# A scratch buffer of the memory stage laid out with the key innermost

## The reference

```
q = (xn @ w_q.T).reshape(b, n, 2, h, kd).transpose(2, 0, 1, 3, 4)
sim = jnp.einsum('pbnhd,hkpd->pbnhk', q, keys)      # 2 sides x 8 heads x 32 keys
s, i = jax.lax.top_k(sim, k)                        # 8 best of each side
all_scores = (sx[..., :, None] + sy[..., None, :]).reshape(b, n, h, k * k)
scores, pk = jax.lax.top_k(all_scores, k)           # 8 best pairs of each head
w_down = key_in[idx];  w_up = key_out[idx]
o = jnp.einsum('bnd,bnhkd->bnhk', inputs, w_down)
o = jax.nn.gelu(o, approximate=False) * jax.nn.softmax(scores, axis=-1)
return jnp.einsum('bnhk,bnhkd->bnd', o, w_up)
```

## Time and profile before

| what | value |
|---|---|
| median of 3 runs | 2622.75 us (2621.32 to 2628.96) |
| the profiled execution, its time | 2621.93 us |
| its span in the profile | 2620.1 us |
| granted TensorE clock over the span | 0.951 of full |
| busy over the span | PE 89%, DVE 79%, ACT 72%, PEld 71%, POOL 32% |

### The profile page before, as it was taken

One profiled execution on the slowest core, in us unless ns is written; L12 is line 12 of the kernel. 1 busy time (PEld: TensorE's weight loads), 2 busy tenths in 40 slices (PEclk: granted clock), 3 DMA queues, 4 the chain that ended last, 5 costly groups with the idle time before them and its releaser, 6 DMA issues.

```text
span 2620.1 us, 95472 instructions
## 1 busy us (share of the span) xinstructions
PE 2343.8 (89%) x34892; PEld 1855.1 (71%) x34892; DVE 2078.6 (79%) x5455; ACT 1887.8 (72%) x3592; POOL 836.3 (32%) x1203
## 2 busy tenths in 40 slices
PE   2999943966999999999889999899899999999999
PEld 1676632645888888888857667566688788888887
DVE  6788889668899999999667777688766777777776
ACT  1888852777688888878467777788567777777776
POOL 1455510336566666666333333233100000000000
PEclk9999975987899999999899999899799999999999
DMA  5000000000000000000020000111011111111111
GB/s 183 1 0 0 0 17 1 1 0 3 2 0 0 0 0 0 0 0 0 3 66 0 0 0 0 36 43 44 30 43 46 49 56 52 57 51 54 52 57 45
DMA packets 56808, 64.82 MB, mean 25 GB/s; under 512 B 7696, under 2 KB 35088, under 8 KB 56592
## 3 DMA queue, kind: packets, MB, share of 16 engines
q1 hardware_dynamic: 56720, 63.65, 7.9%
HBM read 59.17 MB, written 4.46 MB: 24 GB/s over the span
## 4 chain that ended last, share of the span: by engine, by line
PE 68%; DVE 17%; issue 9%; ACT 2%; SPq 1%; DVEq 1%; POOL 1%; ACTq 0%; POOLq 0%; DMA 0%
PE ps L1075 5%; PE ps L1118 5%; PE ps L1103 5%; PE ps L1348 4%; PE ps L1370 4%; PE ps L1372 4%; PE ps L1371 4%; PE ps L1350 4%; PE ps L1349 4%; PE ps L1131 3%; PE ps L1090 3%; DVE work L1829 2%; PE ps L1248 2%; DVE work L1830 2%; DVE work L1836 2%
## 5 line engine op out<-in xcount | busy, mean ns | idle before, releaser
L559 POOL TENSOR_TENSOR work<-work,consts_sb 128x1024 f32<-128x1024 f32 x128 | 245.9, 1921 | 387.8 <-ACT work L727 346.9
L1260 PE MATMUL ps<-work 32*32 32x32 f32 x16384 | 249.5, 224 | 45.7 <-DVE work L1779 31.6
L1260 PEld LDWEIGHTS ps<-work 32*32 32x32 f32 x16384 | 242.2, 145 | 60.3 <-issue 60.3
L1988 DVE TENSOR_TENSOR h_low<-consts_sb,h_up 128x1024 fp32r<-128x1024 f32 x128 | 156.7, 1224 | 116.1 <-ACT h_up L964 116.1
L1586 DVE TENSOR_REDUCE work<-ps 128x8 f32<-128x512 f32 x256 | 169.8, 686 | 86.0 <-PE ps L1075 80.1
L1348 PE MATMUL ps<-a_low,w_up 128*128 128x512 f32 x512 | 205.9, 402 | 0.0
L1370 PE MATMUL ps<-h_low,d_up 128*128 128x512 f32 x512 | 199.9, 390 | 2.3 <-DVE h_low L1988 2.3
L1350 PE MATMUL ps<-a_up,w_low 128*128 128x512 f32 x512 | 200.7, 392 | 0.0
L1349 PE MATMUL ps<-a_up,w_up 128*128 128x512 f32 x512 | 200.6, 392 | 0.0
L1372 PE MATMUL ps<-h_up,d_low 128*128 128x512 f32 x512 | 199.5, 390 | 0.0
L1371 PE MATMUL ps<-h_up,d_up 128*128 128x512 f32 x512 | 199.2, 389 | 0.0
(11 more groups left out here) (297 smaller groups left out, 6271.5 us busy)
## 6 DMA issues: line engine op xcount, KB each, us to landing
gates_spread<-gate_rows SPq DMA_DIRECT2D x128, 256.0 KB, 3.1
ctxT_all<-in_ctxT SPq DMA_DIRECT2D x1, 4096.0 KB, 12.9
work<-in_ctx SPq DMA_DIRECT2D x64, 64.0 KB, 1.7
work<-in_ctxT SPq DMA_DIRECT2D x64, 64.0 KB, 1.7
out<-x_all SPq DMA_DIRECT2D x16, 256.0 KB, 3.5
big<-in_up SPq DMA_DIRECT2D x1, 2048.0 KB, 8.5
consts_sb<-in_consts SPq DMA_DIRECT2D x1, 936.0 KB
w<-in_key_inT SPq DMA_DIRECT2D x1, 512.0 KB, 3.3
```

Of the source, the lines that this page charges most:

```text
L559: pool.tensor_tensor(KX[:, u].rearrange("p b (h k) -> p b h k", h=PER_SET), KC[:, u].unsqueeze(2).to_broadcast([P, 2, PER_SET, SEQ]), own_ ...
L1260: ins = pe.matmul(psW[rows, n // 16, :, n % 16], XT[rows, T.u, :, n], YT[rows, T.u, :, n], start=True, stop=True)
L1988: dve.tensor_tensor(h_low[:, n], hid[n], h_up[:, n].bitcast(F32), ALU.subtract).then_inc(h_split, 1)
```

## The change

`sides` gets another order of its axes. Before, the key was outermost: the value of key k, plane n, head h lay at 64 k + 8 n + h (in floats). After, the key is innermost: it lies at 256 n + 32 h + k. Nothing else changes: the same instructions, in the same order, with the same sizes and waits, read and write the same values through other access patterns.

- `chosen` (L1821) wrote consecutive elements 64 floats (256 bytes) apart; it writes 1024 floats in one run.
- `scaled_one_hots` (L884) wrote consecutive elements 256 bytes apart; it writes runs of 32 floats.
- `turn_sides` (L1829, L1830) read, for each key, two runs of 16 floats; it reads 32 single floats, 32 floats (128 bytes) apart. What it writes is as before.

```diff
         sides = carve(8 * NS)
-        XY = sides.rearrange("p (k n h) -> p n h k", n=8, h=PH)
+        XY = sides.rearrange("p (n h k) -> p n h k", n=8, h=PH)
...
         chosen_terms = XY[:, 2:6].rearrange("p n h k -> p (n h) k")
-        one_hot_sides = sides.rearrange("p (k a r h) -> p a r h k", a=4, r=2, h=PH)[:, 0:4:3]
-        x_side, y_side = [sides.rearrange("p (k a n) -> p k a n", k=NKEY, a=4)[:, :, a:4:2] for a in range(2)]
+        one_hot_sides = sides.rearrange("p (a r h k) -> p a r h k", a=4, r=2, h=PH)[:, 0:4:3]
+        x_side, y_side = [sides.rearrange("p (a n k) -> p k a n", k=NKEY, a=4)[:, :, a:4:2] for a in range(2)]
```

## The result

The changed kernel takes 2674.9 us (median of 4 runs, 2671.7 to 2683.4), against 2622.0 (2617.7 to 2629.0) for the kernel before: ratio 1.0204, 95% interval 1.0177 to 1.0231. It is 2% slower, 53 us, where 33 were forecast. Its profiled execution took 2671.65 us.

A forecast was written before the change was run, and what follows sets the result against it. DVE was taken to bound the memory stage at 10.58 us a tile; - 0.72 (minimum) + 2 x 0.72 (transposes) - 0.10 (relief) = + 0.62, over 52 tiles 32 us, plus about 1 outside: 2655 us, range 2625 to 2695.

The forecast's parts named there:

- The minimum: L1821 on DVE, written in one run instead of scattered: 0.72 us a tile saved by steps, at most 0.81.
- The transposes: L1829 and L1830 on DVE, reading single floats: 0.72 us more each, about 1.95 us long; upper bound 0.89 more.
- The relief: DVE's wait from L1836 to L1770 shrinks as L1788 no longer waits for POOL: 0.21 us every second tile, 0.1 a tile.
- the floor that was foreseen: From L1836 to L1770, where PE's scores L1243 sit between: no less than the first tile's 2.62 us.
- The sum: Minimum, two transposes and relief per tile on DVE: + 0.62 us, 52 times, 32 us.
- The step that failed: POOL and ACT's turn from L628 through L894 and L884: 10.37 us, the shortest possible, fitting into a longer tile.
- The granted clock: PE's clock in the stage: stays at 1.00 from about 690 us on.
- Rival 4: PE's clock drops because PE waits longer: tiles of 12.0 us, 2696 us or more; chance 0.03.
- Rival 1: Reading across is free in a transpose, so POOL and ACT's turn limits: 2605 us, at most down to 2585; chance 0.15.
- The turn of 10.25 us: POOL and ACT's turn, 10.37 us less 0.12 from L884: the limit per tile if transposes read across for free.

The follow-up runs named there:

- e1: Kernel before with only the new write patterns of the minimum and L884, transposes reading as before (wrong keys in the sides): 2621.3 us, ratio 0.9993.
- e2: Kernel before with only the two transposes reading single floats 128 bytes apart, writes as before (wrong keys in the sides): 2696.8 us, ratio 1.0280.
- e3: Changed kernel with pair_floors (L1804) and pair_sums put ahead of top_keys on DVE: 2661.7 us, ratio 1.0154 to the kernel before.
- e4: Changed kernel with a second DVE instruction of 8 floors, into a spare place, right behind L1804: 2700.8 us, ratio 1.0292 to the kernel before.
- e10: Changed kernel with add_memory one turn later on DVE and nothing else: 2698.0 us, ratio 1.0288 to the kernel before.
- m1: Kernel before with transposes and minima of 1024 floats at various steps added behind the memory stage: 1.22 to 1.25 us up to 2 floats, 1.87 to 2.01 from 4.
- e6: Changed kernel with pairs of keys inside sides, planes reordered, minimum in two instructions of 512, IN2 with two places, waits as before: 2620.6 us, ratio 0.9987.
- e8: e6 with add_memory one turn later on DVE: 2606.2 us, ratio 0.9921 to the kernel before.
- one edit alone: The later add_memory, put on e6; this is e8: 2606.2 us, ratio 0.9921 to the kernel before.
- the other alone: e6 using the second place of IN2, so POOL's terms no longer wait for L884 of the tile just before: 2628.2 us, ratio 1.0013.
- together: e6 with both the later add_memory and the second place of IN2 in use: 2585.2 us, ratio 0.9843 to the kernel before.

## Why the prediction was right, and by how much it was not

The direction, the cause and the range held: a scattered read in a transpose is priced like a scattered write, there are two of the one for one of the other, and DVE sets the pace. The size did not: 53 us where 33 were forecast. 2674.9 us lies within 2625 to 2695, but past the 2637 to 2673 to which the price of the transposes alone could lead, and two fifths of the loss come from something that the prediction did not have. That the wide range took it in was luck. Point by point:

- **The minimum**, forecast 0.72 us a tile sooner: by steps 732.49 - 731.36 = 1.13 us against 1.89, so 0.76, and 0.04 more in the step behind it.
- **The transposes**, forecast 1.95 us by duration and 0.72 more by step: 2.00 and 1.97 us, and steps of 1.94 and 1.90 against 2.28 for both together before, so 0.80 and 0.76. The value taken from additions of 64 elements and from the scattered write was 0.04 to 0.08 low, inside its bounds.
- **The relief**, forecast 0.10: from L1836 to L1770 it is now 740.06 - 737.46 = 2.60 us against a mean of 2.73, so 0.13. L1788 runs unhindered, and L1770 waits for L1243 (8.7 us in 46 tiles), the floor that was foreseen.
- **The sum** of these is - 0.80 + 1.56 - 0.13 = + 0.63; measured 0.62, as forecast, in the tiles without a meeting. That it agrees to the hundredth is chance: the transposes cost 0.12 us more than forecast, and the minimum and the relief gave 0.11 more.
- **L884**, forecast 380 ns and eight in 2.4 us: 388 ns and 2.44 us. L1836 is unchanged. L1842, forecast unchanged, is 61 ns shorter; it has 1211 ns in e1 and 1269 in e2, so it depends on how the minimum ahead of it writes.
- **The step that failed** is "it is the shortest turn they can make and fits into a longer tile". It fits, and that was taken to be the end of it. Where a turn that was full gets slack, its start is set by something else. Before, L884 started only when ACT was through with L894. Two rows of the timeline of the kernel before that lie between those of the earlier trace rows:

```profile
1046.26 0.19 DVE L1814 RECIPROCAL work<-work 128x8 f32<-128x8 f32 x1
...
1049.29 0.15 DVE L1804 TENSOR_SCALAR work<-work 128x8 f32<-128x8 f32 x1
```

  L884 came at 1047.36, 1.10 us after L1814 started, and L628 at 1050.04, when L1804 was long over. After, L884 starts 0.26 us after L1814 does (738.76, 739.02). From then on L628 follows L1814 by 2.4 us of L884, 2.85 us in all, while L1804 follows the same L1814 by L1797 and the floor of L1770, 2.88 us in all. The two arrive within 0.05 us of each other in 48 of 64 tiles, and when POOL gets ahead, DVE loses about 1.0 us. The prediction counted POOL only where it was in the way before (L1788). The missing term is 21 meetings x 1.0 = 21 us; 33 + 21 = 54, and 53 was measured between the medians (50 between the profiled executions, whose head was 3 us shorter). e3 takes the meetings away and the loop gives back 18 us; e4 adds a second such instruction and its loop loses 21 more; in e10 nearly every tile meets, and it loses 23. Which tiles meet in one execution rests on hundredths of a microsecond and was not forecast by any of this.
- **The granted clock**, forecast 1.00 from about 690 us: 0.98, and 0.94 in e10. It is 1.00 in e3, where no L1804 is long. DVE sets the pace in all three, and e10's tiles are 11.95 us at 0.94, which the meeting alone explains, so no time is put down to it. Rival 4, tiles of 12.0 us by the clock, did not occur.
- **Rival 1's condition** (reading across for free) was false by m1 and e2. Its number can be judged by e1, e6 and e8, in which the reads are cheap: 2605 was forecast. e1 and e6 took 2621: their usual tile is 10.35 us, and the five slow pairs, each with a fall of the clock and a meeting, cost 10 us. In e8, with the wait for PE gone, the pairs are gone too, and it took 2606. The turn of 10.25 us was right and second in line.

## What to carry to other kernels

When one side of a buffer must be scattered, put pairs of floats inside before choosing which instruction pays: here a step of 8 bytes cost nothing in either direction, and 16 bytes made the instruction take 60% longer. When an engine that was full gets slack, look up what will start it now, and which short instruction with both operands in SBUF comes due on DVE at that same moment as one on POOL. And when a saving does not show, read which wait has appeared and remove it before dropping the edit: on the layout in pairs one edit alone was worth 14 us, the other alone cost 8, and together they were worth 35 (by medians of different sessions; by the ratios 17, 7 and 38).

## What the runs showed of the hardware that was not expected

- The cost of a stride has one step and no slope: 1.22 to 1.25 us for 1024 floats 4 or 8 bytes apart, 1.87 to 2.01 us from 16 to 128 bytes, and slightly less at 64 and 128 bytes (1.89 and 1.90) than at 16 and 32 (1.98 and 2.01).
- A DVE instruction of 8 floats with one input, 0.15 us long, can last until a POOL instruction that started 0.03 to 0.17 us before it ends (1.07 and 0.94 us here). If it starts first, by as little as 0.03 us, neither is held up. With POOL ahead by no more than 0.03 us both outcomes occur. The Trainium skill, SBUF — State Buffer, section Who interferes with whom, says that multiplications by a scalar can enter a mode in which the first to issue keeps the ports shared with POOL for its whole length; the long L1804 agree, down to an instruction of 8 elements; which of the two issued first can't be read from starts 0.03 us apart.
- The granted clock fell to 0.50 of full, the lower of its two levels, for short stretches in e1, in the one shown after PE had waited 1.18 us, and the 16 products of `mixed` took 3.16 us there instead of 2.05. What makes it fall in some pairs of tiles and not in others was not tested. The tile after such a fall is the one in which L1804 met L628, in all five pairs.
